# Issuing the stores of the turned softmax reciprocals from ScalarE instead of SyncE

## What is computed

```
b, s, _ = x.shape
g = H // KVH                       # H, KVH, D = 32, 8, 64
q = (x @ Wq) ...; k = (x @ Wk) ...; v = (x @ Wv) ...
q, k = apply_rope(q, pos), apply_rope(k, pos)
scores = einsum('bhqd,bhkd->bhqk', q, k) / sqrt(D)
scores = where(causal, scores, finfo.min)
attn = softmax(scores, axis=-1)
out = einsum('bhqk,bhkd->bhqd', attn, v) ...
return out @ Wo
```

## Time and profile before

| | |
|---|---|
| median of 3 runs | 1731.78 us (1730.97 to 1733.57) |
| the profiled execution | 1730.82 us |
| its span, first to last instruction | 1729.0 us |
| granted TensorE clock, mean | 0.994 |
| busy: PE / DVE / ACT / POOL | 1675.4 / 1248.8 / 1140.5 / 977.1 us |

### The profile page before, as it was taken

How to read it: one execution, slowest core, us unless ns; L and a number is a source line. 1 busy time by engine, 2 the same in 40 slices (tenths; PEclk the granted TensorE clock), 3 DMA queues, 4 the chain that set the end, 5 groups by cost and what they waited for, 6 DMA issues and landing times. The chain is left out here.

```text
span 1729.0 us, 27586 instructions
## 1 busy us (share of the span) xinstructions
PE 1675.4 (97%) x8993; PEld 1386.7 (80%) x8993; DVE 1248.8 (72%) x2518; ACT 1140.5 (66%) x2315; POOL 977.1 (57%) x822
## 2 busy tenths in 40 slices
PE   6899999999999999999999999889999899999998
PEld 2588888888888888888888888667788688888886
DVE  6788889888889888888888988873333564545433
ACT  4588888888888888888888888863232443323222
POOL 1367777777777777777677777445000245444453
PEclk9999999999999999999999999999999999999999
DMA  7234444445445354454354454456555101001000
GB/s 295 71 106 118 131 122 124 122 112 137 112 117 142 99 132 126 103 139 128 96 148 114 107 132 126 132 152 203 188 187 173 53 1 31 25 13 43 0 31 25
DMA packets 174969, 190.92 MB, mean 110 GB/s; under 512 B 31456, under 2 KB 117736, under 8 KB 174832
## 3 DMA queue, kind: packets, MB, share of 16 engines
q1 hardware_dynamic: 137840, 140.99, 28.7%
q10 hardware_dynamic: 36992, 48.25, 10.2%
HBM read 86.12 MB, written 31.74 MB: 68 GB/s over the span
## 5 line engine op out<-in xcount | busy, mean ns | idle before, releaser
L1102 DVE TENSOR_TENSOR p_lo<-ps_b,p_hi 128x512 fp32r<-128x512 f32 x576 | 395.1, 688 | 103.3 <-ACT p_hi L987 99.5
L987 ACT CAST p_hi<-ps_b 128x512 fp32r<-128x512 f32 x576 | 338.2, 589 | 116.3 <-PE ps_b L889 87.7
L1002 ACT ACTIVATE p<-ps_b,negm 128x640 f32<-128x640 f32 (+7 forms) x512 | 382.9, 752 | 41.2 <-DVE negm L1113 39.8
L1113 DVE CUSTOM_DVE_ANT_0 ps_b<-ps_b,mask_w 128x640 f32<-128x640 f32 (+7 forms) x512 | 385.4, 760 | 21.6 <-PE ps_b L878 17.6
L889 PE MATMUL ps_b<-ident,p 128*128 128x128 f32 x2304 | 345.6, 274 | 9.2 <-DVE p_lo L1102 9.1
L889 PEld LDWEIGHTS ps_b<-ident,p 128*128 128x128 f32 x2304 | 271.9, 140 | 56.1 <-DVE p_lo L1102 13.4
L877 PE MATMUL ps_b<-k_hh,q_hl 128*128 128x512 f32 (+3 forms) x768 | 265.6, 347 | 7.5 <-ACT p L1002 6.8
L903 PE MATMUL ps_b<-p_hi,v_hl 128*128 128x512 f32 x576 | 257.9, 448 | 4.0 <-ACT o_sb L995 3.5
L878 PE MATMUL ps_b<-k_l,q_hl 128*128 128x512 f32 (+3 forms) x768 | 256.2, 347 | 0.0
L904 PE MATMUL ps_b<-p_lo,v_hl 128*128 128x512 f32 x576 | 226.6, 393 | 0.0
L1741 PE MATMUL ps_d<-h_hi,gu 128*128 128x512 f32 x512 | 200.6, 392 | 2.4 <-DVE h_lo L1861 2.4
(11 more groups left out here) (160 smaller groups left out, 3123.6 us busy)
## 6 DMA issues: line engine op xcount, KB each, us to landing
rot_x<-rot_s SPq DMA_DIRECT2D x320, 64.0 KB, 2.0
q_hl<-rot_s SPq DMA_DIRECT2D x128, 128.0 KB, 2.6
q_hl<-rot_x SPq DMA_DIRECT2D x128, 128.0 KB, 2.8
rd_all<-reciprocals SPq DMA_DIRECT2D x128, 128.0 KB, 3.0
o_low<-o_sb ACTq DMA_DIRECT2D x128, 128.0 KB, 2.3
attention_out<-o_sb SPq DMA_DIRECT2D x128, 128.0 KB, 2.5
o_raw<-attention_out SPq DMA_DIRECT2D x32, 512.0 KB, 4.7
wf<-in_L_ffn_w_gate_up ACTq DMA_DIRECT2D x28, 256.0 KB, 3.1
```

The source lines that it names most:

```text
L987: act.copy(p_hi[:, T % P_RING, :], ps[:, T_BANK + T % 2, :]).then_inc(phi_ready, 1)
L1002: act.activation(p_32[:, parity, h, column * P:column * P + nk], s, ACT.Exp, bias=negm[:, k:k + 1], scale=-1.0, accum_out=den[:, parity, k ...
L1102: dve.tensor_tensor(p_lo[:, T % P_RING, :], ps[:, T_BANK + T % 2, :], p_hi[:, T % P_RING, :].bitcast(F32), ALU.subtract).then_inc(plo_read ...
L1113: dve.tensor_tensor_reduce(s, s, mask_w[:, S - nk:S], 1.0, HIGHEST, ALU.add, ALU.min, negm[:, k:k + 1]).then_inc(max_ready, 1)
```

## The change

The four stores of each pair (256 DMAs in all, `save_den`) are issued by ACT instead of SP, and the table SAVES has the place 640 instead of 300. The step stays 9n + 2. On ACT place 640 is behind everything else of the step; its last places before are 620 and 630, the stores and loads of ternary weights. The wait for b_rd_flipped goes with the stores, from SP to ACT.

```diff
-SAVES = Places(own_pairs(2), 300)
+SAVES = Places(own_pairs(2), 640)
...
-            def save_den(g, n):
-                pairs_flip.await_(sp, g, n)
-                for b in range(P // DEN_COLS):
-                    rows = slice(DEN_COLS * b, DEN_COLS * b + DEN_COLS)
-                    sp.dma_start(rden_dram[n % 2, :, rows], rd_turned[rows.start:rows.start + len(ROWS), n % 2, :]).then_inc(rd_out, 16)
...
-                for g, n in body.whole(T, at, SAVES):
-                    save_den(g, n)
...
-            bodies(step, SWAPS, PLACINGS, SAVES, SPREADS, STORES, WEIGHT_LOADS)
+            bodies(step, SWAPS, PLACINGS, SPREADS, STORES, WEIGHT_LOADS)
...
+            def save_den(g, n):
+                pairs_flip.await_(act, g, n)
+                for b in range(P // DEN_COLS):
+                    rows = slice(DEN_COLS * b, DEN_COLS * b + DEN_COLS)
+                    act.dma_start(rden_dram[n % 2, :, rows], rd_turned[rows.start:rows.start + len(ROWS), n % 2, :]).then_inc(rd_out, 16)
...
+                for g, n in body.whole(T, at, SAVES):
+                    save_den(g, n)
...
-                   UNIT_ABS, UNIT_SIGNS, UNIT_STORES, UNIT_LOADS)
+                   UNIT_ABS, UNIT_SIGNS, UNIT_STORES, UNIT_LOADS, SAVES)
```

## The result

| | before | changed |
|---|---|---|
| median | 1732.67 us (1730.97 to 1733.71, 4 runs) | 1750.35 us (1748.97 to 1754.81, 4 runs) |
| ratio | | 1.0106, 95% interval 1.0093 to 1.0118 |
| profiled execution / its span | 1730.8 / 1729.0 us | 1750.5 / 1748.7 us |
| granted clock, mean | 0.994 | 0.989 |

The account below looks back on a forecast made before the run. PE's stream was taken as the bound, with almost no idle time. Pair 0 5.9 + last pair 0.5 - SP relief 1.0 = +5.4 us, giving a 1737.2 us median; range 1731.8 to 1742.0.

Parts of the forecast that it names:

- What bounds the kernel: Attention stage, 100 to 1080 us: PE's stream sets the time, with 1.4 us idle; ACT's extra work counts if it reaches PE.
- the one turn that I had named: PE's turn at 502.68 after pair 0, waiting for DVE's late p_lo: 0.74 us lost per group.
- An issue stops ACT's engine, and work ahead of it covers it: On ACT, an issue between back-to-back instructions delays the next, which starts about 0.1 us after it; earlier queued work hides it.
- the first rival: Nothing reaches PE: ACT's queue runs on behind issues, or they are quick and DVE catches up; 1730.8 to 1733.8 us, chance 0.28.
- Pair 0, 8 x 0.74 = 5.9 us: Pair 0 of each of 8 groups: late flag puts four issues before tile 3's CAST; PE loses 0.74 us each, 4.1 to 10.9 total.
- ACT's "room": ACT's idle time after pair 0, until 501.50: 0.14 us, subtracted from the 1.26 us lateness to give 1.12.
- Pairs 1 to 7 at nothing: The 56 later saves find an old flag; exponentials ahead and PE's slack hide their issues, costing nothing.
- my 0.39 us of exposure: At pair 4 the CAST follows the exponentials after 0.99 us, so up to 0.39 us of the issues is exposed.
- The rival of dear issues: Four ACT issues take 1.9 us or more, or wait for SP's; pair 0 and pairs like 4 pay: 1752 us, chance 0.07.
- The last pair, 0.5 us: At 1151 us, where ACT, DVE and PE wait in turn, the CAST comes 0.77 us late; 0.5 us lost.
- Relief of SP, -1.0 us: SP loses 256 issues and a wait, so its swaps come earlier, removing two PE stalls, together 1.0 us; bounds 0 and 1.4.
- The stall of the earlier trace: At 835 us PE stood for 0.76 us because ACT's copy of rot_c waited on a late swap; forecast to vanish.

Follow-up runs that it names:

- the early flag: Changed kernel with DVE's transpose of pair 0 at its regular place (1, 410), so ACT finds the flag set: 1742.71 us, ratio 1.0055 to the kernel before.
- the second traces: Both kernels profiled once more without a new edit: changed kernel 1749.99 us (ratio 1.0096), kernel before 1731.83 us (one execution).

## Why the prediction was wrong

- **What bounds the kernel:** right. PE's stream had no idle time to win, and what reached PE through ACT and DVE was paid. It was paid at three places, and not at the one turn that I had named.
- **An issue stops ACT's engine, and work ahead of it covers it:** right. In all 8 groups the CAST at pair 0 started 0.10 us after the last issue's end. The reading by which instructions behind the issues run on (the first rival) isn't borne out: by it ACT would have lost nothing, and the gap is 1.43 us. So the rule that the Trainium skill gives in Advanced Engine Details and Errata, Sequencer Loop, doesn't hold here for what stands behind a DMA issue. The cover from ahead is what the early flag shows, 1.43 us down to 0.34.
- **Pair 0, 8 x 0.74 = 5.9 us:** this is the term that was mis-sized; it measured 10.3 by the starts of the turns. Of the missing 4.4, three steps make 8 x 0.39 = 3.1. I took 1.28 us for the four, by SP's row undisturbed; in g = 3 they took 1.46, so the gap was 1.43 and not 1.26 (0.17). I subtracted 0.14 us of ACT's "room", the idle time in the earlier trace rows; it was the hand-over between single instructions and absorbed nothing, as the p_lo at 508.55 shows, which is 1.43 us late (0.14). And I kept 0.06 us of PE's slack for the hand-over; the turn at 502.68 had 0.44 us of slack by the rows, and with 1.43 us of lateness it lost 1.13, so only 0.30 of it was there (0.08). The last 1.3 us is the spread over the groups. 0.8 of it is longer issues: the four took 12.44 us in the eight groups together, 0.76 more than 8 x 1.46, and half of that in g = 6. The other 0.5 stays open. My upper end, with 4 x 0.47 = 1.9 us for four issues, gave 10.9 and comes near the 10.3 by luck: only g = 6 had issues that long.
- **Pairs 1 to 7 at nothing:** wrong. By themselves they cost 5.8 us (0.22 to 0.47%). I looked at pair 1 and pair 4 as typical. A pair with shorter exponentials, such as 6, has nothing long enough ahead of the issues: its CAST was 1.18 us late and the next exponentials 0.52. At pair 4 my 0.39 us of exposure was near what came, 0.42. The rival of dear issues had this step, but with pairs like 4 in the leading part.
- **The last pair, 0.5 us:** too low. The rest of the last group lost 2.65 us in the first traces, in steps at T = 41, 51, 60 and from 67 on, and 1.2 in the second ones. There PE, DVE and ACT wait for each other in turn, by the earlier trace rows none fuller than another, so a late CAST is seen at once. I had priced one of these places.
- **Relief of SP, -1.0 us:** did not come. The stall of the earlier trace rows is there with 0.7 us in the changed kernel's first trace. In the second traces neither the changed kernel nor the one before has it, so this stall comes and goes by itself, and one trace can't price it.
- **The sum.** In the traces the attention stage lost 15.0 us, 9.6 more than the 5.4 of the forecast: 4.4 at pair 0, 1.0 for the relief, and 2.1 + 2.65 - 0.5 = 4.2 at the other pairs. The medians differ by 17.7; the 2.7 beyond the stage is within what the projection varied by (197.4 and 199.1 us in two executions of the kernel before). It is also within what the stage varied by: in the second traces it accounts for 18.3 us, more of them at the other pairs, and the projection for 0.3. So the terms beyond pair 0 are known to some us only. The step that failed is the cost of the issues to PE, too low at pair 0 (5.9 where 10.3 was measured) and put at nothing at the 56 other saves (5.8 by themselves). The range ended at 1742.0, since it took the zeros for most pairs as good; the case of dear issues, 1752, came nearest in time by luck: four issues took 1.9 us at pair 0 in g = 6 alone, and the later pairs that paid were not those like pair 4.

## What to carry to other kernels

In these runs a DMA issue on ACT cost its full issue time against whatever stood behind it in ACT's order, unless ACT was still busy with work from ahead when the sequencer got there (1.43 us of idle time without cover, 0.34 with it). So put the issue where its flag is old and a long instruction stands just before it. Idle tenths summed over a window are not slack: count slack at the one instruction that must not be late, and follow every consumer, since here three of them paid in turn. Cost each repetition from its own row, not from two that look typical, above all where instruction lengths vary along the loop.

## What the runs showed of the hardware

- The issue time of a 1 KB DMA on ACT varies: 0.27 to 1.18 us for one, with a median of 0.32, and 1.31 to 2.38 us for four in a row. The longest four are at pair 3 of g = 7 (timeline of the changed kernel, the last three of them), and at pair 6 of g = 3 four take 2.0 us (timeline of ACT):

```profile
1100.56 2.08 ACTq L980 DMA_DIRECT2D reciprocals<-rd_turned  x3
...
601.45 0.63 ACTq L980 DMA_DIRECT2D reciprocals<-rd_turned  x1
...
602.11 1.34 ACTq L980 DMA_DIRECT2D reciprocals<-rd_turned  x3
603.55 0.59 ACT L985 CAST p_hi<-ps_b 128x512 fp32r<-128x512 f32 x1 [1.26 <-issue]
```

  SP's issues may play a part, but aren't shown to be the cause. Of the 126 that overlap with an issue of SP, 35 took more than 0.34 us, and of the 130 that don't, 22; the medians are 0.318 and 0.317 us.
- Moving 128 issues with their wait to SP, whose own issues had taken 562 of 980 us, cost 66.6 us, and SP stood at that wait for 94.0 us. The time that an in-order queue has left didn't tell here how well it could take a wait.
